# Router scores taken out of the decoder's operands, earlier edge counts, filler matmuls, and a later request for one expert weight

## Chip, core and metric

One core of one Trainium2 chip runs the whole program. The metric is device microseconds of one execution. Engine names are those of the profile: PE (TensorE matmul), PEld (TensorE weight load), DVE (VectorE), ACT (ScalarE), POOL (GpSimd), SP (SyncE, used here as a DMA queue). L1122 is line 1122 of the kernel before.

## What is computed

1250 nodes of 1024 features (10 tiles of 128 rows, the last with 98), 21250 directed edges. Four layers, each added to the stream `x` behind a layer norm:

```python
h = sigmoid(ln(x) @ wenc.T + benc)                       # 500 columns
agg = segment_sum((h @ conv)[src] * edge_weight, dst) + h @ lin.T
x = x + (agg @ wdec.T + bdec)                            # graph layer 1
logits = ln(x) @ wr + br                                 # 4 experts, the best two of each row
x = x + experts_1(ln(x), top2(logits))                   # 1024 -> 512 -> 1024
x = x + gated_relational_layer(ln(x))                    # 8 relations, root, gate
x = x + experts_2(ln(x), argmax(ln(x) @ gate_w.T + b))   # 8 experts, the best one
```

## The kernel before, in words

Every engine has a program of its own; the order is written by hand, and engines meet at semaphores. All weights of the expert and relational layers are split in a high part (ACT, `exp_w[.., k]`, `wh`, `tok_w1h`) and a low part (DVE, the rest), and a product is three matmuls of 512 columns.

**Encoder (0 to 182 us).** DVE sorts the edges by target tile (`sort`, L2058). Between its first and second half it does the layer-norm statistics of all ten tiles (`first_ln`, L2126). ACT normalises (`norm1`), PE transposes (`transpose_x1`), ACT copies back (`take_x1`). The encoder's twelve groups (`q` 0 to 11, L1076) are 8 products each; the groups 8 to 11 are half as wide. PE places 67 of the edge columns in a list by matmul (`permute`, L1059), one behind each product from group 2 on; the other 100 (`SCATTERED`) are written to a table in memory by POOL, one indirect DMA each (L908), and read back by SP (L640). Then PE forms `h @ conv` for ten tiles (L1104), ACT stores it (L1594).

**Edge sums (186 to 415 us).** POOL gathers 176 slots of 128 rows (L917), 16 in flight. PE sums a slot with a one-hot matrix (L1121, L1122), DVE adds it to its tile (L2207). Ten products `h @ lin` lie between the slots (`LIN_AT`).

**Decoder and first router (415 to 507 us).** For each tile PE transposes `agg` (L1126), and forms the 24 matmuls of `decode` (L1128); DVE adds them to `X`, takes statistics; ACT normalises to `ln2_rows`. A tile later PE transposes those rows (`transpose_x2`, L1143), ACT copies them to `XT` (L1635), and two tiles later PE forms 8 products with 4 columns (`route`, L1153); DVE takes the best two three tiles later (`choose0`, L2250). SP stores `ln2_rows` for the gather, and asks for the first weights of experts 1 and 2 only when the last tile is stored and routed (L672 to L676).

**First expert layer (507 to 822 us).** DVE sorts the 2500 pairs into 23 slots, PE turns this into a list (L1185), POOL gathers rows (L925), PE starts at L1203 and L1220. The low parts of the weights are formed by `expert_low` (L2275) in an order written out. The sort does `gate_values` while it waits for PE's counts.

**Relational layer (822 to 2202 us).** Not changed but for its first transpose.

**Second router and expert layer (2202 to 2465 us).** After the last gated tile the route is `transpose_x4`, `route4`, `sort`, the list, four row gathers (L1000), and 17 slots of `up` and `down`. SP asks for expert 0's first and second weights (L845, L851), then for slot 1's first weights, bias, second weights and second bias (L855 to L858), then for slot 2's first weights (`next_w1(0, 0)`, L875). SP takes its instructions in order.

Of the kernel before, what the change touches and what calls it, by code (L numbers as in the profile page):

```python
# [21 lines left out]
F32 = mybir.dt.float32  # L22
# [8 lines left out]
P = 128  # L31
# [16 lines left out]
SCATTERED = 100  # L48
# [56 lines left out]
LN1_AFTER = {0: (4, 5), 1: (6,), 2: (7,), KE: (8,), KE + 1: (9,)}  # L105
# [14 lines left out]
T_AGG = T_LN1 + 2 * NT  # L120
# [12 lines left out]
V_ROUTE = V_DEC + 2 * NT  # L133
V_PRE0 = V_ROUTE + 1
# [44 lines left out]
def build(nc, a, out):  # L179
    ctx = ExitStack()  # L180
    with ctx:
# [162 lines left out]
        hot1 = place("hot1", "hot", [P, RING, P], BF16)  # L344
        hotr = sb("hotr", [P, RING, REL], BF16)
# [12 lines left out]
        b_route = sb("b_route", [P, E0])  # L358
        w_route2 = sb("w_route2", [P, KD, E1])
# [81 lines left out]
        sum_iota = banks[4][:, 0:P]  # L441

# [79 lines left out]
        u2_out = os_kept[1:4] + [(x_in[1], 16), (x_in[2], 16)]  # L522
        t3_out = [(parts_in[k], 32 * len(range(k, NT, 4))) for k in range(4)] + os_kept[0:1]
        c21_out = [(edges_in, 64), (consts_in, 16 * 7), (list_in, 16)]
# [11 lines left out]
        x4_full, xT4_ready, X4 = exp_x_full, exp_xT_ready, 2 * NT + 2 * ESLOTS  # L536
# [68 lines left out]
        def _(sp):  # L605
# [4 lines left out]
            for i in range(2):  # L610
                lo, hi = (0, 4) if i == 0 else (4, NT - 1)
                sp.dma_start(X[:, lo:hi, :], tiles[:, lo:hi, :]).then_inc(x_in[i], 16)

            sp.wait_ge(pad_zero, 1)
            sp.dma_start(X[0:LAST, NT - 1, :], a["x"][(NT - 1) * P:N_NODES, :]).then_inc(x_in[2], 16)
# [9 lines left out]
            sp.dma_start(w0, wide(a["encT"])).then_inc(s0, 16)  # L625
            w1, s1 = unit(UNIT_CONVLIN)
# [9 lines left out]
            sp.wait_ge(room_zero, 1)  # L636
            sp.dma_start(list_dram[0:P * SLOTS0, :].rearrange("(p s) c -> p (s c)", s=SLOTS0), room[:, 0, 0:2 * SLOTS0]).then_inc(list_zero, 16)
# [19 lines left out]
            def load_hidden(s):  # L657
                sp.wait_ge(*hid_stored(s))
                if s < 2:
                    sp.wait_ge(exp_x_full, 2 * NT + 2 * (ESLOTS - 2) + 2)  # L660
                else:
                    sp.wait_ge(exp_hl_ready, 1 + s - 1)
# [5 lines left out]
            first_weights(0, raw[:])  # L668
            for m in range(NT):
# [186 lines left out]
            load_b1(e, 1)  # L856
            load_w2(e, new, 1)
# [25 lines left out]
        def _(pool):  # L883

            pool.memset(X[96:P, NT - 1, :], 0.0).then_inc(pad_zero, 1)
# [14 lines left out]
            pool.memset(room[:], 0.0).then_inc(room_zero, 1)  # L900
# [2017 lines left out]
```

## Time and profile before

| | us |
|---|---|
| median of 3 executions | 2465.64 (2461.29 to 2466.44) |
| the profiled execution's own time | 2467.0 |
| its span in the profile | 2465.1 |
| mean granted TensorE clock | 0.974 |

| engine | busy us | share |
|---|---|---|
| PE | 2315.0 | 94% |
| PEld | 1772.4 | 72% |
| DVE | 1648.0 | 67% |
| ACT | 987.9 | 40% |
| POOL | 858.3 | 35% |

The span is one execution on the core. A busy share is a mean over stages with different limits, so it says which engine is full on the whole and not what a stage waits for.

### The profile page before, as it was taken

The numbers are of one execution on the slowest core, as the hardware profiler recorded it, in microseconds if no ns is written. First come the engines' busy times: TensorE is split into PE (matmuls) and PEld (weight loads), VectorE is DVE, ScalarE is ACT, GpSimd is POOL, SyncE is SP. The second block draws the span as 40 slices with busy tenths as digits, with TensorE's granted clock in tenths as the row PEclk, the third lists the DMA queues.
The fourth block names the chain that finished last, engine by engine and source line by source line (L and its number), as shares of the span: only waits on it lengthen the run. The fifth ranks groups of instructions, "written<-read, shape, count | busy, mean of one in ns | idle before, by whom it ended". The sixth has DMA issues, their size and how long they took to land.

```text
span 2465.1 us, 30737 instructions
## 1 busy us (share of the span) xinstructions
PE 2315.0 (94%) x10060; PEld 1772.4 (72%) x10060; DVE 1648.0 (67%) x2581; ACT 987.9 (40%) x1745; POOL 858.3 (35%) x835
## 2 busy tenths in 40 slices
PE   6998998979999799999999999999999898986998
PEld 3553334868877587888888888887778676875886
DVE  9726777465664576554554555558889889976656
ACT  3112223344343443122121222237889896444333
POOL 2767774011112256545400000034445551103443
PEclk9999999979999899999999999999999998988999
DMA  4027776155454575435435345368678894458884
GB/s 161 2 80 205 209 207 183 64 210 150 116 182 163 179 263 196 151 128 200 141 119 210 122 145 177 123 225 269 213 263 294 293 342 148 158 181 290 306 307 156
DMA packets 195410, 464.06 MB, mean 188 GB/s; under 512 B 29576, under 2 KB 30344, under 8 KB 195288
## 3 DMA queue, kind: packets, MB, share of 16 engines
q1 hardware_dynamic: 98248, 213.30, 24.8%
q0 software_dynamic: 63632, 188.10, 23.9%
q10 hardware_dynamic: 33408, 61.13, 6.6%
q8 instruction: 65, 1.06, 0.2%
q14 instruction: 57, 0.47, 0.1%
HBM read 362.09 MB, written 105.97 MB: 190 GB/s over the span
## 4 chain that ended last, share of the span: by engine, by line
PE 84%; DMA 6%; DVE 5%; issue 2%; ACT 2%; POOL 1%; DVEq 0%; ACTq 0%; SPq 0%; POOLq 0%
PE pair L1367 9%; PE pair L1368 9%; PE pair L1369 9%; PE pair L1122 5%; PE pair L1085 3%; PE pair L1104 3%; PE pair L1385 3%; PE pair L1388 3%; PE pair L1405 2%; PE pair L1407 2%; PE pair L1406 2%; PE pair L1253 2%; PE pair L1254 2%; PE pair L1255 2%; PE pair L1220 2%
## 5 line engine op out<-in xcount | busy, mean ns | idle before, releaser
L1536 ACT ACTIVATE sq_h<-quad 128x512 fp32r<-128x512 f32 x196 | 122.9, 634 | 453.6 <-PE pair L1369 448.8
L1367 PE MATMUL pair<-sq_h,xh 128*128 128x512 f32 x700 | 273.3, 390 | 2.7 <-DVE sq_l L2547 2.7
L1368 PE MATMUL pair<-sq_h,xl 128*128 128x512 f32 x700 | 273.0, 390 | 0.0
L1369 PE MATMUL pair<-sq_l,xh 128*128 128x512 f32 x700 | 272.9, 390 | 0.0
L976 POOL DMA_INDIRECT rows_y<-y_rows,l_row x184 | 196.1, 1066 | 212.8 <-PE pair L1388 189.2
L2635 DVE SCALAR_TENSOR_TENSOR low_y<-rows_y,l_inv,high_y 128x1024 fp32r<-128x1024 f32 x184 | 233.9, 1284 | 41.8 <-ACT high_y L1536 41.6
L1536 ACT ACTIVATE high_y<-rows_y,l_inv 128x1024 fp32r<-128x1024 f32 x184 | 210.3, 1143 | 35.8 <-PE pair L1388 22.1
L953 POOL DMA_INDIRECT inv_ring<-inv_count,at_ring x184 | 189.4, 1029 | 70.9 <-issue 52.4
L2547 DVE TENSOR_TENSOR sq_l<-quad,sq_h 128x512 fp32r<-128x512 f32 x196 | 131.4, 696 | 96.7 <-ACT sq_h L1536 95.9
L917 POOL DMA_INDIRECT XT<-h_rows,l_src x176 | 169.0, 960 | 66.2 <-issue 34.4
L1122 PE MATMUL pair<-XT,XN 128*128 128x504 f32 x352 | 178.9, 633 | 0.0
L1367 PEld LDWEIGHTS pair<-sq_h,xh 128*128 128x128 f32 x700 | 131.7, 188 | 31.0 <-DVE sq_l L2547 3.6
L2207 DVE TENSOR_TENSOR U<-pair,U 128x512 f32 x176 | 121.4, 690 | 46.6 <-DVE U L2207 22.3
L967 POOL COPY X<-bias_u 128x1024 f32<-128x1024 f32 x10 | 10.7, 1127 | 406.4 <-PE pair L1369 406.4
L1369 PEld LDWEIGHTS pair<-sq_l,xh 128*128 128x128 f32 x700 | 131.8, 188 | 27.5
L1368 PEld LDWEIGHTS pair<-sq_h,xl 128*128 128x128 f32 x700 | 131.8, 188 | 27.4
L1385 PE MATMUL pair<-high_y,hot 128*128 128x512 f32 x368 | 117.4, 400 | 18.0 <-DVE low_y L2635 17.9
L1405 PE MATMUL pair<-wh,xh 128*128 128x512 f32 x320 | 125.8, 393 | 2.8 <-DVE wl L2662 2.5
L1407 PE MATMUL pair<-wl,xh 128*128 128x512 f32 x320 | 124.9, 390 | 0.0
L1406 PE MATMUL pair<-wh,xl 128*128 128x512 f32 x320 | 124.9, 390 | 0.0
L1536 ACT ACTIVATE XN<-hot,l_w 128x128 f32<-128x128 bf16 x176 | 57.0, 390 | 161.4 <-DVE hot L2194 161.0
L908 POOL DMA_INDIRECT list_rows<-e_rows x100 | 96.2, 962 | 70.8 <-DVEq L2150 40.7
(402 smaller groups left out, 5583.0 us busy)
## 6 DMA issues: line engine op xcount, KB each, us to landing
quad<-in_L_gnn_weight SPq DMA_DIRECT2D x28, 1024.0 KB, 5.6
xh<-sum_parts SPq DMA_DIRECT2D x14, 1280.0 KB, 7.6
xl<-sum_parts SPq DMA_DIRECT2D x14, 1280.0 KB, 11.2
y_rows<-u ACTq DMA_DIRECT2D x70, 256.0 KB, 2.3
tok_raw<-in_L_ffn_w SPq DMA_DIRECT2D x8, 2048.0 KB, 11.4
tok_raw<-in_L_ffn_w SPq DMA_DIRECT2D x16, 1024.0 KB, 13.5
x_rows<-X SPq DMA_DIRECT2D x20, 512.0 KB, 6.5
pair<-pair_rows SPq DMA_DIRECT2D x18, 512.0 KB, 5.9
```

Of the source, the lines that this page charges most:

```text
L953: pool.indirect_dma_start(inv_ring[:, k:k + 1], None, inv_rows, bass.IndirectOffsetOnAxis(ap=at_ring[:, 0, k:k + 1], axis=0)).then_inc(inv ...
L976: pool.indirect_dma_start(rows_y[s % RING1][:], None, y_rows, bass.IndirectOffsetOnAxis(ap=l_row8[:, s:s + 1], axis=0)).then_inc(y_in[s % ...
L1122: mm(sum_bank[s % 4][:, 0:EMBC], hot[:, s % RING, :], rows_h2[:, s % RING0, 0:EMBC], start=True, stop=True).then_inc(slot_summed, 1)
L1367: mm(o, high[:, k, :], sq_h[:, k, :], start=(k == 0), stop=False)
L1368: mm(o, low[:, k, :], sq_h[:, k, :], start=False, stop=False)
L1369: last = mm(o, high[:, k, :], sq_l[:, k, :], start=False, stop=(k == KE - 1))
L1385: mm(o[:, cols], hot_s, high[:, cols], start=first, stop=False)
L1405: mm(o, xh[:, m, k, :], wh[:, k, :], start=(k == 0), stop=False)
L1406: mm(o, xl[:, m, k, :], wh[:, k, :], start=False, stop=False)
L1407: last = mm(o, xh[:, m, k, :], wl[:, k, :], start=False, stop=(k == KD - 1))
L1536: return nc.scalar.activation(dst, src, func, **kw)
L2635: v.scalar_tensor_tensor(low_y[s % RING1][:], rows_y[s % RING1][:], l_inv[:, s:s + 1], high_y[s % 3][:].bitcast(F32), ALU.mult, ALU.subtra ...
```

## The change

- **Edge list:** 108 instead of 100 columns are scattered by POOL, 59 instead of 67 go through PE. PE's columns start at group 3. POOL's wait for the list's columns is looser.
- **Start:** the node tiles are asked for as tile 0, tiles 1 to 3, (zeroed list, encoder weights), tiles 4 to 8, tile 9. Only tiles 0 to 3 have their statistics inside the sort; 4 to 6 follow the scatter's release, 7 to 9 stand among the columns. ACT's square roots of tiles 5 to 9 now stand between sigmoids. `slot_groups` moves behind the columns.
- **Scores, linear part of `x`:** the router's 4 columns are copied into unused columns 500 to 503 of the encoder's weights, so that the encoder's fourth column group also gives `ln(x) @ wr`. ACT copies that group out (`stage_sc`), PE transposes it (`turn_scores`), ACT keeps `route_x1`.
- **Scores, decoder part:** while the first rows are awaited PE transposes the decoder's weights (32 transposes, 8 copies by ACT), and during slots 16 to 47 forms `wdec.T @ wr` in 32 small matmuls. `decode` then adds 8 matmuls of 8 columns to each tile (high and low parts). DVE adds both parts, and turns them into logits with the tile's mean and root (`choose0`, one tile later).
- **Gone:** `transpose_x2`, its copies to `XT`, `route`.
- **Weights:** expert 2's first weights are asked for together with expert 0's; expert 1's when all tiles are stored. The sort does two `expert_low` pieces where it did `gate_values`; `gate_values` goes behind `expert_x_low(1)`, and all of expert 1's low parts behind it.
- **Filler:** `keep_busy(n)` is n float32 matmuls of 128x128 whose result nobody reads: 16 behind the pair counts (L1180), 12 ahead of `expert_rows(0)`, 16 ahead of `transpose_x3(0)` once the first pairs are in, 9 ahead of and 5 behind `transpose_x4(9)`, 30 behind the second sort's counts (L1469), 30 ahead of `transpose_rows(0)` (L1521).
- **Second expert layer:** slot 1's second weights are asked for when the rows of slots 0 and 1 have landed.

```diff
-SCATTERED = 100
+SCATTERED = 108
-LN1_AFTER = {0: (4, 5), 1: (6,), 2: (7,), KE: (8,), KE + 1: (9,)}
+LN1_AT = {(1, 7): 4, (2, 3): 5, (2, 7): 6, (3, 3): 7, (5, 7): 8, (6, 7): 9}
+COLUMNS_FROM = 3
+STATS_AT, SCALES_AT = {2: (7,), 8: (8,), 10: (9,)}, {6: (7,), 18: (8, 9)}
+SCORES_AT = (KE + 2, 2 * KE)
+SUMS_AT, DEC_SCORES_AT, PARTS_AT = 8, 16, 52
...
             sp.wait_ge(slot_summed, RING0 + SLOTS0)
             first_weights(0, raw[:])
+            first_weights(2, exp_raw[0][:])
...
-            sp.wait_ge(exp_x_full, 2 * NT)
             first_weights(1, exp_raw[1][:])
-            sp.wait_ge(a_full, A_ROUTE + NT)
-            first_weights(2, exp_raw[0][:])
...
             load_b1(e, 1)
+            sp.wait_ge(*tok_rows_here(0))
+            sp.wait_ge(*tok_rows_here(1))
             load_w2(e, new, 1)
...
+            def keep_busy(times, bank=banks[0]):
+                for _ in range(times):
+                    mm(bank[:, 0:P], before[:], ones[:], start=True, stop=True)
+            def turn_scores(g):
+                pe.wait_ge(a_read, A_ENC + KE * (g + 1))
+                transpose4(T_SC + g, [stage_sc[:, q * P:(q + 1) * P] for q in range(TOKG[g][1] // P)])
...
+                    if q == KE - 1:
+                        pe.wait_ge(a_read, 1)
-                        if q >= A_ENC + 2:
+                        if q >= COLUMNS_FROM:
                             next_column()
-                    transpose_x1(LN1_AFTER.get(q, ()))
+                        if (q, k) in LN1_AT:
+                            transpose_x1((LN1_AT[q, k],))
+                    if q in SCORES_AT:
+                        turn_scores(SCORES_AT.index(q))
...
+            pe.wait_ge(w_in[0], 32)
+            for r in range(KD):
+                ...
+                for c in range(KE):
+                    last = nc.tensor.transpose(turn_bank[r % 3][:, c * P:(c + 1) * P], dec_raw[:, c, r // 4, (r % 4) * P:(r % 4 + 1) * P], ident[:])
+            def dec_scores(n):
+                c, k = divmod(n, KD)
+                mm(dec_route_bank[:, c * E0:(c + 1) * E0], dec_turned[:, k, c * P:(c + 1) * P], w_route[:, k, :], start=(k == 0), stop=(k == KD - 1))
...
                         mm(o, agg_h[:, m % 2, k, :], dec_h[:, k, h, :], start=(k == 0), stop=False)
+                        if h == 0:
+                            mm(score_bank[m % 2][:, 0:2 * E0], agg_h[:, m % 2, k, :], dec_route[:, k, :], start=(k == 0), stop=False)
                         mm(o, agg_l[:, m % 2, k, :], dec_h[:, k, h, :], start=False, stop=False)
+                        if h == 0:
+                            score = mm(score_bank[m % 2][:, 0:2 * E0], agg_l[:, m % 2, k, :], dec_route[:, k, :], start=False, stop=(k == KE - 1))
...
-                if m >= 1:
-                    transpose_x2(m - 1)
-                if m >= 2:
-                    route(m - 2)
-            route(NT - 2)
-            transpose_x2(NT - 1)
-            route(NT - 1)
...
+            takes_after = {1: (4,), 2: (5, 6), 5: (8,), 6: (9,)}
+            norms_after = {1: (5, 6), 2: (7,), 3: (8, 9)}
...
+                    if c == KE - 1:
+                        if g >= 1:
+                            act.wait_ge(t_full, T_SC + g)
+                        copy(stage_sc[:, 0:n], enc_bank[q % 4][:, 0:n])
...
+            def take_score(m):
+                dve.wait_ge(a_full, A_ROUTE + m + 1)
+                link(v.tensor_tensor(route_x1[:, m, :], score_bank[m % 2][:, 0:E0], route_x1[:, m, :], ALU.add))
+                v.tensor_tensor(route_x1[:, m, :], score_bank[m % 2][:, E0:2 * E0], route_x1[:, m, :], ALU.add).then_inc(a_read, 1)
             def choose0(m):
-                v.tensor_tensor(logits[:, m, 0:E0], score_bank[m % 2][:, 0:E0], b_route[:], ALU.add).then_inc(a_read, 1)
+                dve.wait_ge(rstd_tile_ready, NT + m + 1)
+                link(v.scalar_tensor_tensor(route_tmp[:, m, :], route_consts[:, 0:E0], nmr[:, m:m + 1], b_route[:], ALU.mult, ALU.add))
+                link(v.scalar_tensor_tensor(logits[:, m, 0:E0], route_x1[:, m, :], rstd[:, m:m + 1], route_tmp[:, m, :], ALU.mult, ALU.add))
...
-            expert_low(in_raw, 2, range(2, KD))
-            expert_low(in_place[1], 1, range(0, 4))
+            expert_low(in_raw, 2, range(4, KD))
             expert_x_low(0)
             expert_x_low(1)
-            expert_low(in_place[1], 1, range(4, KD))
+            gate_values()
+            expert_low(in_place[1], 1, range(KD))
```

## Rows read from the trace of the kernel before

**Rows 1.** The page: the chain that ended last, by engine.
```profile
PE 84%; DMA 6%; DVE 5%; issue 2%; ACT 2%; POOL 1%; DVEq 0%; ACTq 0%; SPq 0%; POOLq 0%
```
**Rows 2.** Timeline of the encoder (start us, busy us, engine, line, count, [idle before <-releaser]).
```profile
29.32 9.12 PE L1085 MATMUL pair<-XT,W 128*128 128x512 f32 x16 [0.78 <-ACT XT L1536]
...
38.52 1.28 ACT L1581 ACT_TABLE_LOAD   x1 [6.47 <-PE pair L1085]
...
41.14 1.06 PE L1038 MATMUL pair<-ident,XN 128*128 128x128 f32 x8 [1.82 <-ACT XT L1536]
...
42.04 7.03 PE L1085 MATMUL pair<-XT,W 128*128 128x512 f32 x16
...
50.64 0.75 PE L1061 MATMUL pair<-room 128*128 128x352 f32 x2
...
147.84 34.57 PE L1104 MATMUL pair<-W,U 128*128 128x512 f32 x80 [0.61 <-issue]
...
179.72 0.25 DVE L2177 TENSOR_SCALAR l_row<-l_row 128x176 f32<-128x176 int32 x1
```
**Rows 3.** POOL's scatters (L908) and gathers (L917): duration ns, first and last start.
```profile
L908 POOL DMA_INDIRECT list_rows<-e_rows x100: 957/962/1125, 47.3 to 172.7; - x100
...
L917 POOL DMA_INDIRECT XT<-h_rows,l_src x176: 945/949/1208, 186.5 to 407.9; - x176
```
**Rows 4.** Busy time in windows (PE, PEld, DVE, ACT, POOL, granted clock, DMA share, GB/s).
```profile
300.00:320.00 20.00, 19.33 (x57) 7.32 (x56) 15.21 (x26) 6.25 (x18) 15.31 (x16) 1.00 0.71 209
...
460.00:480.00 20.00, 20.00 (x122) 17.51 (x121) 10.53 (x30) 6.42 (x11) 0.00 (x0) 1.00 0.20 79
...
2228.00:2240.00 12.00, 3.36 (x11) 2.73 (x12) 1.38 (x2) 1.20 (x2) 4.70 (x5) 0.50 1.04 394
```
**Rows 5.** Timeline of the decoder's first and last tiles.
```profile
418.34 0.50 PE L1138 MATMUL pair<-dec_h,agg_h 128*128 128x512 f32 x1 [1.39 <-DVE agg_l L2043]
...
496.00 1.04 PE L1150 MATMUL pair<-ident,ln_rows 128*128 128x128 f32 x8
...
496.87 3.63 PE L1158 MATMUL pair<-w_route,XT 128*128 128x4 f32 x32
```
**Rows 6.** Timeline from the last decoder product to the first gathered rows.
```profile
498.41 0.16 DVE L2056 SCALAR_TENSOR_TENSOR nmr<-mv,rstd 128x1 f32<-128x1 f32 x1
...
502.39 3.57 PE L1158 MATMUL pair<-w_route,XT 128*128 128x4 f32 x16 [0.69 <-ACT XT L1536]
...
506.48 0.16 DVE L2255 FIND_INDEX8 top_at<-top,logits 128x8 uint32<-128x8 f32 x1
...
521.30 0.94 POOL L925 DMA_INDIRECT exp_rows<-xn_rows,exp_list  x1 [112.47 <-DVEq L2341]
```
**Rows 7.** Timeline of the first expert slots.
```profile
502.51 3.88 SPq L650 DMA_DIRECT2D exp_raw<-in_L_ffn_w  x2
...
512.63 4.27 ACT L1536 ACTIVATE exp_w<-exp_raw 128x512 fp32r<-128x512 f32 x8 [4.62 <-DMA exp_raw<-in_L_ffn_w]
...
528.63 0.79 PE L1220 MATMUL pair<-exp_w,exp_x 128*128 x1 [0.96 <-DVE exp_x L2353]
...
534.17 0.69 DVE L2353 TENSOR_TENSOR exp_x<-pair,exp_x 128x512 fp32r<-128x512 f32 x1 [2.74 <-ACT exp_x L1536]
```
**Rows 8.** Timeline: first product behind the pairs' gather, in the relational layer.
```profile
841.62 0.80 PE L1308 MATMUL pair<-wh,xh 128*128 128x512 f32 x1 [2.00 <-DVE xl L2043]
```
**Rows 9.** Timeline of the second expert layer's start.
```profile
2213.38 4.26 ACT L1536 ACTIVATE tok_w1h<-tok_raw 128x512 fp32r<-128x512 f32 x8 [6.40 <-DMA tok_raw<-in_L_ffn_w]
...
2226.98 0.95 POOL L991 DMA_INDIRECT tok_rows<-xn_rows,tok_list  x1 [43.89 <-DVEq L2800]
...
2235.22 1.94 PE L1482 MATMUL pair<-ident,tok_rows 128*128 128x128 f32 x8 [10.31 <-DMA tok_rows<-xn_rows,tok_list]
...
2238.58 0.80 PE L1491 MATMUL pair<-tok_w1h,tok_xh 128*128 128x512 f32 x1 [1.41 <-DVE tok_xl L2816]
...
2256.12 4.27 ACT L1536 ACTIVATE tok_w1h<-tok_raw 128x512 fp32r<-128x512 f32 x8
```

More of the change, by code:

```diff
@@ L119 @@
 T_LN1 = 0
-T_AGG = T_LN1 + 2 * NT
+T_SC = T_LN1 + 2 * NT
+T_DEC = T_SC + len(TOKG)
+T_AGG = T_DEC + KD
+SCORES_AT = (KE + 2, 2 * KE)
+ROUTE_AT = EMB
+SUMS_AT, DEC_SCORES_AT, PARTS_AT = 8, 16, 52
+assert DEC_SCORES_AT >= SUMS_AT + BATCH + 4 and PARTS_AT >= DEC_SCORES_AT + KE * KD
 T_LN3 = T_AGG + NT
@@ L132 @@
 V_DEC = 1
[L133 to L134 removed]
+V_PRE0 = V_DEC + 2 * NT
 V_LIST0 = V_PRE0 + 1
@@ L1096, in _ @@
             pe.wait_ge(a_read, last_enc)
+            turn_scores(len(TOKG) - 1)
             w = unit(UNIT_CONVLIN)
@@ L1594, in _ @@
                 act.dma_start(h2_dram[m * P:(m + 1) * P, :], OS[:, k, :]).then_inc(os_out[k], 16)
+            for r in range(KD):
+                act.wait_ge(t_full, T_DEC + r + 1)
+                copy(dec_turned[:, r, :], turn_bank[r % 3]).then_inc(t_read, 1)
             for s in range(SLOTS0):
+                if s == PARTS_AT:
+                    act.wait_ge(slot_summed, RING0 + DEC_SCORES_AT + KE * KD)
+                    copy(dec_route[:, :, 0:E0], dec_route_bank.rearrange("p (c e) -> p c e", e=E0))
                 if s % BATCH == 0:
@@ L1625, in _ @@
             agg_high(0)
-            for m in range(NT + 2):
+            for m in range(NT + 1):
                 if m + 1 < NT:
@@ L2117, in _, with first_stats, first_tiles @@
             v.tensor_scalar(tok_pad[:], tok_id[:], float(N_NODES + 1), 100.0, ALU.is_ge, ALU.mult)
+            def first_stats(m):
+                if m in (0, 1):
+                    dve.wait_ge(x_in[m], 16)
+                if m == 4:
+                    dve.wait_ge(x_in[2], 32)
+                ln_stats(m).then_inc(x_tile_ready, 1)
+            def first_tiles():
+                for m in range(4):
+                    first_stats(m)
+                    if m >= 1:
+                        tile_scale(m - 1, 0)
+                tile_scale(3, 0)
             dve.wait_ge(edges_in, 64)
@@ L2260, in _ @@
                     agg_low(m + 1)
-                if m >= 3:
-                    choose0(m - 3)
+                if m >= 1:
+                    choose0(m - 1)
                 for h in range(2):
@@ L2287, in _ @@
                 v.tensor_scalar(pair_id[:, k * NT:(k + 1) * NT], tok_id[:], float(TOP0), float(k), ALU.mult, ALU.add)
-            for m in range(NT - 3, NT):
-                last = choose0(m)
-            link(last)
-            v.sem_inc(v_read, 1)
+            link(choose0(NT - 1))
             link(v.tensor_copy(top_f[:], top_at[:]))
@@ L2302, in gate_values @@
                 link(v.tensor_tensor(gsm[:, 4, :], gsm[:, 3, :], gsm[:, 1, :], ALU.mult))
-            sort(pair_key[:], E0, PT, pair_hot[:], pair_cum[:], pair_pos[:], v_bank[V_PRE0 % 2], V_PRE0, pair_tmp[:], pair_far[:], gate_values, least=E0)
+            sort(pair_key[:], E0, PT, pair_hot[:], pair_cum[:], pair_pos[:], v_bank[V_PRE0 % 2], V_PRE0, pair_tmp[:], pair_far[:], lambda: expert_low(in_raw, 2, range(0, 2)), least=E0)
             link(v.tensor_copy(pair_posi[:], pair_pos[:]))
```

202 lines of the change are left out of this document (125 added, 77 removed).

## Prediction

> **What bounds the kernel now.** I read the chain by engine first: 84% of it is PE [rows 1], so a stretch can be shortened only where PE has less to do, or where something else is in the chain. The timeline then shows three stretches that the change touches. Up to 182.4 us PE runs through: the encoder from 29.3, and 80 matmuls of `h @ conv` that begin at 147.84 and take 34.57 [rows 2]. From 186.5 to 407.9 POOL issues 176 gathers, one each 221.4/175 = 1.265 us [rows 3]; PE is 19.3 of 20 us busy in a window of it, DVE 15.2 [rows 4], so the gathers bound it and PE has about 3% to spare. From 418.3 to 496.0 PE is full while DVE has 10.5 of 20 and ACT 6.4 [rows 4, 5]: PE bounds the decoder. Behind it come chains with PE nearly idle, to the first expert product at 528.63 [rows 6, 7], and from the last router to 2238.58 [rows 9].
>
> **The front.** Products of 512 columns lie 7.03/16 = 0.44 us apart, so a column of the list (two matmuls of 352) costs 0.59 [rows 2]; eight fewer save 4.7. ACT normalises tile 0 after two statistics, not three; I estimate 1.5 earlier, of a first product at 29.32 that ended a wait for ACT [rows 2]. Against it: before, PE stood 1.82 at the transpose behind group 0, for a table load of 1.28, a sigmoid and a copy [rows 2]. Now the same wait lies behind group 2, once more with a load, and with one more copy ahead of it (2.9), and about 0.8 ahead of tile 5: 1.9 more. Three `turn_scores` are 10 transposes of 1.06/8 = 0.13 [rows 2], with waits for the sigmoid and an extra copy by ACT: 2.3. Sum: -4.7 -1.5 +1.9 +2.3 = **-2.0** (from -3.5, if the loads fall into idle time, to +2, if each of six switches between root and sigmoid is met). Scatters: 108 end 8 x 1.27 = 10.1 later by their own pace [rows 3], and start 6 layer norms and the slot numbers earlier, more than that. The list was ready at 180.0, h2 at 182.4 [rows 2], so the gathers hang on h2: they start at 184.5.
>
> At the roots and sigmoids the rows show 1.28 us for a table load and nothing behind it [rows 2]. [...]
>
> **Edge sums: 0.** The pace of 1.265 stays. The 32 transposes (4.2 us at 0.13) and 8 copies of ACT lie in the 4 us between the first gather's issue and its landing, and in what follows; the decoder's weights are asked for behind the scatters, near 171. The 32 score products are 64 matmuls near 0.11, 7 us, in a stretch where PE has 3% of slack: it falls behind by some 6, which 16 rows in flight (20 us) hide, and which the other 128 slots give back. If it isn't given back, up to +5.
>
> **Decoder.** Removed before its last product: 8 times `transpose_x2` at 496.87 - 496.00 = 0.87, and 7 routes at 3.63/2 = 1.8: 19.6. Added: 80 small matmuls. Their price isn't in the trace; the nearest are the route's of 4 columns in the same place, 3.63/32 = 0.113 [rows 5]: 9.0. Ends: 0.02 (hidden in its neighbour), and the 0.22 that the same route takes at 502.39 (3.57/16) [rows 6]. Sum **-10.6** (-18 to -2). Per tile PE then needs about 6.8, DVE by my count 5.7 (its 5 us of before, two additions, one step more in `choose0`), so PE stays the bound, and its waits stay short. ACT loses 1.1 per tile.
>
> **Behind the last product (496.0).** Before, its rows were transposed and routed, the route ended at 502.39 + 3.57 = 505.96, the choice at 506.64: 10.6. Now the choice needs only the statistics, whose scale is there at 498.57 [rows 6], two additions and `choose0`: about 1.25 more, 3.8 in all. **-6.8.** The sort itself is the same, its two `expert_low` pieces end where PE's counts come: +0.2. The filler behind the counts (16 of two matmuls at 0.11 to 0.22, about 5) fits in the 6 that PE waits there. So the first row gather goes from 521.3 to 521.3 - 2.0 - 10.6 - 6.8 + 0.2 = 502.1.
>
> **First expert slots.** Expert 1's weights can only be asked for when the last tile is stored, some 6.5 behind the last product: 483.4 + 6.5 = 489.9. Before, the same request went out at 502.51 and was there at 512.63, 10.1 later; ACT takes 4.27 for each of two experts [rows 7]: 489.9 + 10.1 + 8.5 = 508.5, and only then `exp_x`, which the rows want at 507.7. About +1. DVE then does 8 pieces and `gate_values` between its second and its third `exp_x`; it idled 2.74 there before [rows 7]. Together **+1.5** (0 to +4). The 23 slots behind are PE's own and unchanged.
>
> **First relational product: 0.** At 841.62 it waits for DVE, not for PE [rows 8]; faster transposes leave it there. The filler of some 5 us starts with the pairs and ends with the first normalised tile: -1.9 to +0.8.
>
> **Second expert layer.** The filler around `transpose_x4(9)` shortens the route by up to 2, but DVE's sort does two low pieces that wait for ACT, and ACT for a load that lands at 2213.38 [rows 9]: 0. The gathers are issued at 2226.98 in both. [...] With the 2 MB of second weights out of the way I take 5, so they are there at 2232. [...] Queued behind SP's new wait are the second weights, a bias and slot 2's first weights: two requests of 2 MB from 2233 on at 394 GB/s [rows 4], beside 1.5 MB of rows, are there by 2249; slot 2's are used at 2256.1 - 2.9 = 2253.2. That cover is 4 us.
>
> **Sum.** -2.0 -10.6 -6.8 +0.2 +1.5 -2.9 = -20.6. The profiled execution took 2467.0 (span 2465.1), so it would take 2446.4; it stood 1.4 above the median of 2465.64, which gives **2445.0**.
>
> **Rivals.**
> - *Front and start both lose:* the table switches and score transposes eat the columns' gain (+2 in place of -2), expert 1's weights come 2.5 later, DVE's packed order holds slot 2. For it: ACT gets six more loads, and its race at 508 has no slack. Against: ACT was idle 6.5 us around the first load. -20.6 + 4 + 2.5 = -14: 2451.5. Chance 0.20.
> - *Each switch costs its load twice:* the wait behind group 2 and the one ahead of tile 5 grow by 1.3 each, -18: 2447.7. Against: the next ACT row begins when the load ends [rows 2]. [...] Chance 0.08.
> - *Small matmuls nearly free:* they hide under their 512-column neighbours, DVE's 5.7 becomes the tile time less waits, and the filler gains more. -20.6 - 8 = -28.6: 2437. For it: five of six neighbours are long. Chance 0.13.
> - *The filler doesn't do what it is for:* the clock still stands at half where real work starts, and only the earlier landing counts, with the rows behind the filler: -2.9 becomes 0. 2448. Chance 0.12.
> - [...] If DVE's chain (decoder sum, statistics, score, scale, choice) is nearer 9 than 5.7 a tile, PE idles over 2 us in each; behind 0.7 us of idleness and short matmuls the route at 502.39 ran at half rate [rows 6], while at 418.34, behind 1.4, products ran at full rate [rows 5]. Ten tiles of 6.8 would take twice as long: -20.6 + 68 - some overlap = +40, 2505. [...] Against: DVE's count. Chance 0.03.
>
> **Numbers.** Forecast 0.44, rivals as above. The bounds of the unknown costs, not all at once, reach 2436 to 2456, and that takes in all but the slower case. A measurement of this kernel tells 0.2% (about 5 us) from no change. All cases but the last and a tail of the first (0.02, within 0.2%) are faster by more: 0.95, 0.02, 0.03.
>
> **What would show it.** First gather near 184.5 and the last 221 later; decoder tiles 6.8 apart; last decoder product to first expert gather in 18.7, not 25.3; first expert product 18 to 19 earlier than 528.63; first `tok_rows` landing in 5, and PE at 0.23 spacing at once. Wrong would be: gathers that wait for sums (PE the bound there), PE idle between decoder tiles, `exp_x` behind ACT's weights by over 3, slot 2 of the last layer waiting for its weights.

## The result and the profile after

The kernel after takes 2443.14 us in the median of 4 runs (2441.12 to 2448.11), the kernel before 2466.04 beside it (2461.29 to 2469.06): ratio 0.9922, 95% interval 0.9905 to 0.9939, 22.9 us by the medians. Forecast were 2445.0 and 2436 to 2456. The profiled execution took 2441.12, its span is 2439.3, mean granted clock 0.984 (0.974 before). The spans differ by 25.8.

The first table cuts them at events that both traces have. "Measured" is how much each stretch of after is longer than that of before; the last column is my term for it.

| stretch | before | after | measured | forecast |
|---|---|---|---|---|
| start to first row gather of the edge sums | 186.51 | 179.57 | -6.9 | -2.0 |
| first to last gather of the edge sums | 221.37 | 223.54 | +2.2 | 0 |
| last gather to first decoder product | 10.46 | 10.27 | -0.2 | 0 |
| that to the last decoder sum read | 77.86 | 69.53 | -8.3 | -10.6 |
| that to the last choice of experts | 10.28 | 3.31 | -7.0 | -6.8 |
| choice to first expert gather | 14.82 | 14.57 | -0.2 | +0.2 |
| gather to first expert product | 7.33 | 7.91 | +0.6 | +1.5 |
| first expert product to first gather of layer 2 | 1698.35 | 1695.48 | -2.9 | 0 |
| that gather to the end | 238.12 | 235.12 | -3.0 | -2.9 |
| sum | | | -25.8 | -20.6 |

The sum was missed by 5.2: by 4.9 in the first row, while the misses of the other rows (+2.2, +2.3, -2.9, -0.9 and smaller ones) nearly cancel. In after PE has 78% of the chain by engine, DMA 9% (84% and 6% in [rows 1]).

**Front.** Timeline of after (start us, busy us, engine, line, operation, count, idle before and its releaser). PE's row of 139.69 answers to 147.84 in [rows 2], POOL's first gather to [rows 3].

```profile
4.46 0.25 DVE L2203 TENSOR_SCALAR U<-U 128x167 int32<-128x167 int32 x1 [0.42 <-DMA U<-in_edge_weight]
...
35.85 1.28 ACT L1641 ACT_TABLE_LOAD   x1
...
37.15 0.69 ACT L1641 ACTIVATE U<-pair,b_enc 128x512 f32<-128x512 f32 x1
...
44.36 1.09 PE L1058 MATMUL pair<-ident,XN 128*128 128x128 f32 x8 [0.78 <-ACT XN L1589]
...
50.24 1.06 PE L1058 MATMUL pair<-ident,XN 128*128 128x128 f32 x8 [1.36 <-ACT XT L1581]
...
139.44 0.41 PE L1058 MATMUL pair<-ident,stage_sc 128*128 128x128 f32 x2 [1.04 <-ACT U L1641]
139.69 34.50 PE L1138 MATMUL pair<-W,U 128*128 128x512 f32 x80
...
168.55 0.43 SPq L661 DMA_DIRECT2D dec_raw<-in_decT  x1
...
174.85 0.33 ACTq L1661 DMA_DIRECT2D h_rows<-OS  x1
...
177.54 5.38 PE L1156 MATMUL pair<-ident,dec_raw 128*128 128x128 f32 x32 [3.36 <-DMA dec_raw<-in_decT]
...
179.57 0.97 POOL L937 DMA_INDIRECT XT<-h_rows,l_src  x1 [12.55 <-DMA h_rows<-OS]
```

DVE begins on the edges at 4.46, not at 6.66; PE waits for ACT at 44.36, 50.24 and 139.44 (and once for 0.34); the last rows of `h @ conv` are stored at 174.85 and gathered from 179.57, 4.7 later, where before it was 186.51 - 183.08 = 3.4.

**Decoder and choice.** Timeline of after, its last decoder tiles, and windows at its first (columns as in [rows 4]).

```profile
469.69 0.69 DVE L2370 TENSOR_TENSOR X<-X,pair 128x512 f32<-128x512 f32 x1 [1.32 <-PE pair L1204]
...
476.53 0.69 DVE L2370 TENSOR_TENSOR X<-X,pair 128x512 f32<-128x512 f32 x1 [1.31 <-PE pair L1204]
...
480.19 0.69 DVE L2370 TENSOR_TENSOR X<-X,pair 128x512 f32<-128x512 f32 x1 [0.29 <-PE pair L1204]
...
482.91 0.69 DVE L2370 TENSOR_TENSOR X<-X,pair 128x512 f32<-128x512 f32 x1 [1.30 <-PE pair L1204]
...
486.22 0.16 DVE L2358 FIND_INDEX8 top_at<-top,logits 128x8 uint32<-128x8 f32 x1
```

```profile
413.00:415.00 2.00, 1.62 (x5) 1.38 (x6) 0.93 (x2) 0.00 (x0) 0.00 (x0) 0.67 0.92 310
415.00:417.00 2.00, 2.00 (x7) 1.68 (x6) 0.00 (x0) 0.00 (x0) 0.00 (x0) 0.50 1.01 372
```

Half tiles without small matmuls are 482.91 - 480.19 = 2.72 long, one with 8 of them 480.19 - 476.53 = 3.66: 0.117 for each, where 0.113 was forecast. A tile that also transposes the next sums takes 476.53 - 469.69 = 6.84, 6.8 by the forecast. The first tile ran at half clock for about 3.7 us, where before, behind the same wait of 1.39, it ran at full rate [rows 5].

**First expert slots and second expert layer.** Timelines of after; they answer to [rows 6, 7] and [rows 9].

```profile
489.21 0.38 SPq L669 DMA_DIRECT2D exp_raw<-in_L_ffn_w  x1
...
498.82 8.43 ACT L1581 ACTIVATE exp_w<-exp_raw 128x512 fp32r<-128x512 f32 x16 [6.58 <-DMA exp_raw<-in_L_ffn_w]
...
507.15 1.06 ACT L1581 ACTIVATE exp_x<-pair 128x512 fp32r<-128x512 f32 x2
...
508.70 0.79 PE L1258 MATMUL pair<-exp_w,exp_x 128*128 x1 [1.92 <-DVE exp_x L2454]
...
2204.05 9.34 PE L1066 MATMUL pair<-ones,before 128*128 128x128 f32 x60 [2.96 <-DVEq L2901]
2204.18 0.95 POOL L1011 DMA_INDIRECT tok_rows<-xn_rows,tok_list  x1 [44.34 <-DVEq L2901]
...
2211.67 1.49 SPq L839 DMA_DIRECT2D tok_raw<-in_L_ffn_w  x2
...
2213.22 1.04 PE L1526 MATMUL pair<-ident,tok_rows 128*128 128x128 f32 x8
...
2215.83 0.50 PE L1535 MATMUL pair<-tok_w1h,tok_xh 128*128 128x512 f32 x1 [1.57 <-DVE tok_xl L2917]
...
2224.73 0.47 PE L1535 MATMUL pair<-tok_w1h,tok_xh 128*128 128x512 f32 x1 [1.62 <-DVE tok_w1l L2933]
```

The weights of expert 1 were asked for at 489.21 (489.9 forecast) and their pieces end at 507.15 with `exp_x` right behind them, the race as drawn, 1.3 earlier. In the second layer the filler ends at 2213.4, though SP, which waits for the rows of both slots, was let go by 2211.67.

### The profile page after: what moved, and what is told of

The parts are those of the page before. It is cut to its first block, busy times and chain, and to the rows that moved or that the text cites. A ratio compares the mean times of both kernels' runs of the same rounds, so it can differ in the third digit from the quotient of the medians.

```text
span 2439.3 us, 31100 instructions
## 1 busy us (share of the span) xinstructions
PE 2322.1 (95%) x10228; PEld 1791.2 (73%) x10228; DVE 1639.1 (67%) x2596; ACT 993.3 (41%) x1747; POOL 864.7 (35%) x843
## 4 chain that ended last, share of the span: by engine, by line
PE 78%; DMA 9%; DVE 5%; issue 3%; ACT 2%; POOL 2%; DVEq 0%; SPq 0%; ACTq 0%; POOLq 0%
PE pair L1408 9%; PE pair L1409 9%; PE pair L1410 9%; PE pair L1179 5%; DMA tok_x<-x_rows,tok_list 5%; PE pair L1426 3%; PE pair L1429 3%; PE pair L1138 3%; PE pair L1115 3%; PE pair L1446 3%; PE pair L1447 3%; PE pair L1448 3%; PE pair L1291 2%; PE pair L1292 2%; PE pair L1293 2%
## 5 line engine op out<-in xcount | busy, mean ns | idle before, releaser
L928 POOL DMA_INDIRECT list_rows<-e_rows x108 | 103.9, 962 | 59.5 <-issue 32.3
```

## The experiments

Each run has a median of 4 timed runs (10 in the first), and a ratio to the kernel before from the same chip. Single executions of one kernel lie up to 12 us apart, so the traces' stretches carry most verdicts, and medians only what is over 3 us. Lines in the rows are those of each variant.

**1. POOL's zeroing of `room`.** The change shortens it from 4096 columns to 352, in a line that the diff above leaves out, and my forecast has no term for it. In the kernel before:

```diff
-            pool.memset(room[:], 0.0).then_inc(room_zero, 1)
+            pool.memset(room[:, 0, 0:2 * SLOTS0], 0.0).then_inc(room_zero, 1)
```

> The kernel before, with one edit: POOL zeroes only the 352 columns of `room` that are copied to the list, not all 4096. Theory A (two engines slow each other): the two small DVE operations that took 3.50 and 3.31 us beside the 3.51 us memset take under 0.4 each, DVE starts on the edges at about 4.5 instead of 6.66, and the first encoder product comes at 27.2 instead of 29.32; the kernel is about 2 us faster. Rival B (DVE waited for the edge loads, which land near 4.4 or 6.6 whatever POOL does): DVE's edge work starts at 6.6 still, and the time is unchanged.

Timeline of the kernel before, and of this one:

```profile
3.14 3.51 POOL L900 MEMSET room<- 128x4096 f32 x1
3.23 3.50 DVE L2116 TENSOR_SCALAR before<-iota_free,iota_part 128x128 f32<-128x128 f32 x1 [2.05 <-POOL ident L898]
3.43 3.31 DVE L2117 TENSOR_SCALAR tok_pad<-tok_id 128x10 f32<-128x10 f32 x1
```

```profile
3.13 0.39 POOL L900 MEMSET room<- 128x352 f32 x1
3.23 0.38 DVE L2116 TENSOR_SCALAR before<-iota_free,iota_part 128x128 f32<-128x128 f32 x1 [2.04 <-POOL ident L898]
...
4.21 0.25 DVE L2121 TENSOR_SCALAR U<-U 128x167 int32<-128x167 int32 x1 [0.59 <-DMA U<-in_edge_weight]
```

Measured: theory A for the mechanism. The two DVE operations fall from 3.50 and 3.31 to 0.38 and 0.19, edge work starts 2.45 earlier, the first product comes at 27.76 (1.6 earlier), the first gather at 184.16 (2.4), the last decoder sum 1.65 earlier. Not all of the 2.4 is the memset: the encoder of this execution also began at full rate, its first 16 products taking 2.0 less than in [rows 2], and the last store of `h @ conv` was gathered from 4.7 behind it and not 3.4.

```profile
27.76 7.10 PE L1085 MATMUL pair<-XT,W 128*128 128x512 f32 x16 [0.78 <-ACT XT L1536]
```

But the choice comes at 506.43 against 506.48, and the time is 2463.44, ratio 0.9993 (0.998 to 1.0007). In its trace the end of the router stands at half rate for longer than in [rows 5, 6] (the last 32 products ahead of them took 4.62, not 3.63, and the last transposes 1.95, not 1.35): the 1.65 us went there. In the kernel after that piece of PE work is gone.

The reverse, in the kernel after: a second memset behind `ident`.

```diff
+            pool.memset(room[:, 1:4, :], 0.0).then_inc(more_zero, 1)
...
             v.sem_inc(scatter_ready, 1)
+            dve.wait_ge(more_zero, 1)
```

> The kernel after, with a second memset of POOL over the other 3072 columns of `room`, put where the large one was before. Theory A: the memset takes 2.6 us, the two small DVE operations last as long as it, edge work begins 1.5 to 2 later than 4.46, the first encoder product comes at 27 instead of 25.30, 1.5 to 2 us lost in all. Rival B: DVE is untouched by it, first product at 25.3, no loss.

Measured: memset 2.66 at 3.58, DVE's two operations 2.65 and 2.46, edge work from 6.24, first product at 26.91, `h @ conv` from 141.29, first gather at 180.96: 1.8, 1.6, 1.6 and 1.4 later than after. The median, 2442.17, doesn't show it. So the memset is worth 1.6 us at the first product in either direction, and 1.4 at the first gather where nothing else changed; in the total it is below what I can tell.

**2. The second layer's filler and SP's wait.** Four variants of the kernel after. The first leaves out the last `keep_busy(30)`, the third and fourth make it 15; the second and fourth leave out SP's wait:

```diff
-            sp.wait_ge(*tok_rows_here(0))
-            sp.wait_ge(*tok_rows_here(1))
...
             pe.wait_ge(tok_list_ready, 1)
-            keep_busy(30)
+            keep_busy(15)
```

> The kernel after without the last filler, 30 times two passes of PE behind the list of the second expert layer. Theory A (the filler ends after the rows have landed, so it costs as much as it gives): the transposes start when the rows land, about 7.4 us behind the first gather instead of 9.0, but cold, 1.94 long, and slot 0's first products at 0.43 spacing; the first product stands where it stood, 11.6 behind the gather, and slot 1's first product comes 1.3 to 1.6 later; 1.5 us slower in all. Rival B (the filler is worth what I forecast, 0.95 for the transposes and 1.5 for the products, and costs nothing): 2.5 slower. Rival C (the earlier rows alone count): no change or 1 faster.

> The kernel after, without SP's wait for the rows of slots 0 and 1 ahead of slot 1's second weights. Theory A (the rows land about 1 us later, and the filler, which ends 1.6 after them, hides that): the first rows land 8 us behind the gather instead of about 7.4, slot 0's transposes stay at 9.0 behind it, and the time is within 0.5 us of the kernel after. Rival B (my forecast: rows take 5 with the wait and 8 without): start unchanged at the first slot, since the filler covers it, but the rows of slot 1 late by 1 or 2, so up to 1 us slower. Rival C (the wait costs, since the second weights come late): up to 1.5 us faster, by what PE waits at slot 1's first products now.

> The kernel after with 15 in place of 30 fillers in front of the second expert layer. Without them the transposes began 5.59 us behind the first gather, with 30 of them 9.04. Theory A (the filler overshoots the rows by 3.4, and a shorter one keeps the clock as well): the filler takes 5.5, the transposes start 5.6 to 6 behind the gather and are 1.04 long, first product 8.3 behind it (11.65 now), slot 0's products at 0.23 spacing, slot 1's first product 17.1 to 17.5 behind the gather (20.55 now); 3 us faster than the kernel after. Rival B (15 are too few to raise the clock by the time real work starts): the transposes start at 5.6 but slot 0 runs at 0.43 spacing, slot 1 at 20.5 behind the gather, no gain.

> The same shorter filler, and SP's wait ahead of slot 1's second weights taken away. Theory A (the wait lets the rows land in 5.6 instead of about 8, and this is now uncovered): transposes 8 to 8.5 behind the gather, 2.5 later than with the wait, so 2 to 2.5 us slower than the kernel with 15 fillers and the wait. Rival B (the rows' landing is not what the second weights delay): same start as with the wait, same time.

PE's timelines behind the first gather: without filler (gather at 2206.36), with 15 (2209.77; the fourth row is DVE's), and with 15 and no wait (2204.72):

```profile
2211.95 1.94 PE L1526 MATMUL pair<-ident,tok_rows 128*128 128x128 f32 x8 [8.67 <-DMA tok_rows<-xn_rows,tok_list]
2215.30 0.80 PE L1535 MATMUL pair<-tok_w1h,tok_xh 128*128 128x512 f32 x1 [1.41 <-DVE tok_xl L2916]
```

```profile
2209.65 6.07 PE L1066 MATMUL pair<-ones,before 128*128 128x128 f32 x30 [2.96 <-DVEq L2901]
2215.55 1.08 PE L1526 MATMUL pair<-ident,tok_rows 128*128 128x128 f32 x8
2218.20 0.50 PE L1535 MATMUL pair<-tok_w1h,tok_xh 128*128 128x512 f32 x1 [1.57 <-DVE tok_xl L2917]
...
2226.27 4.89 DVE L2933 TENSOR_TENSOR tok_w1l<-tok_raw,tok_w1h 128x512 fp32r<-128x512 f32 x8
...
2227.10 0.47 PE L1535 MATMUL pair<-tok_w1h,tok_xh 128*128 128x512 f32 x1 [1.62 <-DVE tok_w1l L2933]
```

```profile
2213.02 1.97 PE L1524 MATMUL pair<-ident,tok_rows 128*128 128x128 f32 x8 [2.51 <-DMA tok_rows<-xn_rows,tok_list]
2216.40 0.80 PE L1533 MATMUL pair<-tok_w1h,tok_xh 128*128 128x512 f32 x1 [1.41 <-DVE tok_xl L2915]
```

All columns are us behind the first gather; "last slot" is the first `down` product of slot 16.

| fillers | SP waits | transposes | slot 1's first product | slot 2's first product | last slot | end |
|---|---|---|---|---|---|---|
| 0 (before) | no | 8.24 | 21.99 | 36.1 | 222.0 | 238.1 |
| 0 | yes | 5.59 | 20.59 | 34.8 | 220.7 | 235.1 |
| 30 | no | 8.74 | 20.25 | 32.8 | 218.6 | 234.8 |
| 30 (after) | yes | 9.04 | 20.55 | 34.8 | 220.6 | 235.1 |
| 15 | yes | 5.78 | 17.33 | 29.8 | 215.7 | 231.8 |
| 15 | no | 8.30 | 22.12 | 36.1 | 222.0 | 238.1 |

Up to slot 1's first product each half alone gives 1.4 to 1.7 us and both together give 1.4 as well, for the 30 fillers last 9.3 and the rows, with SP's wait, 5.6. With 15, which end as the rows land, the two add up to 4.7, and without the wait all is lost again: PE idles 2.5 and is cold (granted clock 0.50, transposes 1.97). The mechanism of theory A held in all four, its sizes in two. In the first the first product came 2.7 earlier than in after, slot 0 at half rate (its first products 0.43 apart, 0.23 in after) took that back, and nothing was lost, where 1.5 were forecast. In the fourth the loss is 6.3 and not 2.5: 4.8 at slot 1's first product, since I left out that the clock falls too, and the rest behind it.

To the end the gains look like 3, 3, 3 and 6.3, but two more things are in these numbers, and neither was planned. The first is another meeting of POOL and DVE. From slot 1's first product to slot 2's it takes 12.5 in the second and third variant, and 14.0 to 14.2 in the others, before and after included. In after POOL adds a bias to `tok_x` while DVE forms the low parts of slot 1's first weights: one of DVE's eight pieces lasts 2.87 instead of 0.68, all eight 7.08 instead of the 4.89 of the variant with 15, and PE waits 1.46. With 15 fillers these pieces end before that addition begins; with 30 and no wait they do too, for its rows land later. In the kernel before and in the fourth variant it falls on the low parts of the second weights, and one piece of these lasts 2.65 to 2.79. In the second and third variant it falls on them as well, but there POOL's addition is what lasts longer (5.63 and 7.01), and DVE keeps its pace (4.89); what decides between the two isn't shown. Timeline of after:

```profile
2223.91 7.08 DVE L2933 TENSOR_TENSOR tok_w1l<-tok_raw,tok_w1h 128x512 fp32r<-128x512 f32 x8
...
2226.78 2.46 POOL L1031 TENSOR_TENSOR tok_x<-tok_x,U 128x1024 f32<-128x1024 f32 x1 [3.09 <-DMA tok_x<-x_rows,tok_list]
...
2229.84 0.50 PE L1535 MATMUL pair<-tok_w1h,tok_xh 128*128 128x512 f32 x1 [1.46 <-DVE tok_w1l L2933]
```

The second is the clock in the last slot. From its first `down` product, always behind a wait of 2.05 or 2.06, to the end it is 14.5 in nine of the fourteen traces and 16.1 in five (before, three of these variants, and the first of experiment 7). The kernel before has both (14.5 in experiment 1), and so has the shorter filler with the wait, so it is chance. Windows in it, of before and of after (columns as in [rows 4]):

```profile
2450.00:2453.00 3.00, 3.00 (x9) 2.33 (x8) 0.00 (x0) 0.00 (x0) 1.01 (x1) 0.50 0.05 8
```

```profile
2426.00:2429.00 3.00, 3.00 (x15) 2.48 (x14) 0.69 (x1) 0.00 (x0) 1.01 (x1) 1.00 0.03 3
```

The medians, 2443.91, 2440.82, 2441.62 and 2445.22, are too coarse for this: on one chip the first two differ by 3.1, where their traces differ by 0.4 from the gather on, and on another the last two by 3.6, where it is 6.3. The intervals of their ratios overlap.

**3. The decoder's weights.** They were asked for at 168.55, behind the scatters. Here at 138.08:

```diff
+            sp.wait_ge(a_full, A_H2)
+            sp.dma_start(dec_raw[:]..., wide(a["decT"])).then_inc(w_in[UNIT_DEC % 2], 16)
             sp.wait_ge(scattered, 16 * SCATTERED)
...
-            sp.wait_ge(a_full, A_H2)
-            sp.dma_start(dec_raw[:]..., wide(a["decT"])).then_inc(w_in[UNIT_DEC % 2], 16)
```

> The kernel after with the decoder's weights asked for before SP waits for the scatters, at about 140 instead of 168.5. Theory A (the first gather waits for the last rows of `h @ conv`, whose store is held up behind the 2 MB of weights; it came 4.7 behind the store where the weights landed last and 2.9 where the store was issued after them): the gather comes 2.4 to 3 behind the last store, at 177.3 if the encoder starts warm (h @ conv from 139.7) and 179.5 if cold (from 141.8); up to 2.3 us faster. Rival B (a store takes 3 to 4.7 there by its own chain of stores): gather stays 4.7 behind the store. In both the list is not the bound, ready at 171.7.

Timeline of this variant, the last store of `h @ conv` and the first gather:

```profile
174.50 0.33 ACTq L1661 DMA_DIRECT2D h_rows<-OS  x1
...
177.37 0.98 POOL L937 DMA_INDIRECT XT<-h_rows,l_src  x1 [10.29 <-DMA h_rows<-OS]
```

Measured: theory A. The store at 174.50 is gathered from at 177.37, 2.9 later. The three variants of experiment 2 whose encoder began cold bear it out without any edit there: their store left as the weights landed, and was gathered from 2.9 later too. The median is 2437.87, ratio 0.9892 (0.9872 to 0.9913), whose interval overlaps that of after, so the gain is read from the store and the gather alone. So in the kernel after the front's end is set by 2 MB of weights that land first.

**4. No filler at all.** `keep_busy` does nothing.

> The kernel after without any of its six fillers. Theory A (each filler only warms what follows it): counts to first expert gather unchanged (14.6 us from the choice) or up to 1.5 longer, by the list's products at half rate; first expert product within 1 of where it is; last route of the second router 1.2 slower, at half rate; list of the second layer 1 slower; start of slot 1 as without the last filler. Together 2 to 4 us slower than the kernel after. Rival B (the fillers are worth nothing, since DVE's chain sets these places): within 1 us of it.

Measured: 2448.73, ratio 0.9931; its profiled execution 2452.48. Choice to first expert gather 14.56, to the first expert product 7.89: both as in after, so up to there the fillers buy nothing. The last router tile of layer 2 is back at half rate (PE's timeline of this variant; its 16 score products take 3.58 as in before, 1.85 in after):

```profile
2194.29 3.58 PE L1478 MATMUL pair<-w_route,xT 128*128 128x8 f32 x16 [0.69 <-ACT xT L1580]
...
2211.19 2.30 PE L1516 MATMUL pair<-tok_perm_val,tok_perm_lane 128*128 128x18 f32 x10 [9.94 <-DVE tok_perm_val L2891]
```

That is 1.2 from the norm to the choice, and 1 at the list. From the gather to the end it is 235.15, as without the last filler. Its first gather came at 182.43, 7.0 behind the store, for the decoder's weights took 12.4 us to land: that is not the fillers' doing. The median is 5.6 above that of after, but from another chip; by the ratios to the kernel before, 0.9931 and 0.9922, it is 2.2, with overlapping intervals. A's 2 to 4 fits, and isn't shown by the total.

**5. The list's columns.** `SCATTERED = 100` in the kernel after.

> The kernel after with 100 scatters, so 67 columns of the list on PE instead of 59. Theory A (8 columns of 0.59 lie on the way to `h @ conv`): from the first encoder product to the first of `h @ conv` 4.7 more (119.1 if warm at the start, 121.4 if cold; 114.4 or 116.8 with 108); the scatters end 10 earlier, so the decoder's weights are asked for at 158 and have landed long before the last store: the first gather comes 2.9 behind the store and not 4.7, so 2.9 us later in all and not 4.7. Rival B (columns hide in the waits for ACT): 1 to 2 more only.

Measured: from the first product to `h @ conv` 146.57 - 25.00 = 121.57, against 116.7 to 116.8 in the three executions with 108 scatters whose encoder began cold too: 4.8. Theory A, 4.7 forecast. The store at 181.74 was gathered from at 184.60, 2.9 behind. The median is 2446.02, ratio 0.9914 (0.9898 to 0.9931), beside the 0.9922 of after: the total doesn't show the loss.

**6. What the score products cost the edge sums.** 28 of 32 are left out, so the router sees another sum and picks other experts; only the gathers are read.

```diff
-                if DEC_SCORES_AT <= s < DEC_SCORES_AT + KE * KD:
+                if DEC_SCORES_AT <= s < DEC_SCORES_AT + KE * KD and (s - DEC_SCORES_AT) % KD == 0:
```

> The kernel after with 4 of the 32 score products in the edge sums; 28 are left out, so the router scores lack 7/8 of the decoder's part and the choice of experts is another. Only the stretch from the first to the last gather is read. It took 221.4 in the kernel before and 223.2 to 223.5 in the kernel after and its variants. Theory A (64 small passes of PE put its sums behind, and the gathers wait for a free row twice): two long gaps between gathers, near 200 and 217, shrink from 1.6 and 2.1 to 1.4 or less, and the stretch is 222.3 or less. Rival B (the transposed decoder weights and the copies that share ACT set it): unchanged, 223.3.

Measured: 223.01, so neither: the gap at 217 shrinks from 2.1 to 1.7, the one at 199 to 1.46, and those two are about 0.5 of the 2.2. The whole stretch can't show that, for with all 32 products it lay between 222.87 and 223.70. The kernel before with the small memset took 222.33 for its own gathers, so 1 of the 2.2 comes without the change. The rest wasn't found.

**7. A version that beats both.** First the decoder's weights early and 15 fillers, then also these:

```diff
-SCATTERED = 108
+SCATTERED = 110
...
+            keep_busy(3)
             pe.wait_ge(agg_ready, 1)
...
                 if m + 1 < NT:
                     transpose_agg(m + 1)
+                if m == 0:
+                    keep_busy(5)
                 decode(m)
...
-            keep_busy(12)
+            keep_busy(24)
```

> The kernel after with the decoder's weights asked for at about 140 and with 15 in place of 30 fillers ahead of the second expert layer. Theory: the two gains add, 2.2 from the gathers (the first at 177.4 to 179.6, 2.9 behind the last store) and 3.3 behind the second layer's first gather (231.8 us from it to the end, not 235.1): about 5.5 us faster than the kernel after, 2437 to 2438, ratio to the kernel before 0.989 to 0.990. Rival (what lies between takes back what comes early): 2440 or more, with both stretches as said and the stretch between them longer.

> As the kernel with both edits, and three more: 110 scatters (two columns of the list fewer on PE, 1.2 us), 3 and 5 fillers around the first transposes of the decoder, and 24 in place of 12 ahead of the first expert rows. Theory A: first gather 1.2 earlier (the list is ready at about 174.5, ahead of the rows at 176); the decoder's stretch is 67.9 and not 69.5; the first expert product's neighbours lie 0.23 apart from the start instead of 0.43 for 3.5 us, 1.8 gained; 3 us faster than the kernel with the two edits. Rival B (the clock behind 1.9 us of idleness is low whatever stood ahead): slot 0 at 0.43 again, gain only 1.2. Rival C (the filler overshoots): slot 0's transposes later than 4.5 behind the first gather.

Measured: 2441.06, ratio 0.9882 (0.9864 to 0.9900), and 2433.94, ratio 0.9859 (0.9835 to 0.9883). Against the 0.9922 (0.9905 to 0.9939) of the kernel after, from another chip, the second is faster with room between the intervals; those of the first are 0.0005 apart, too little to hang anything on. The intervals of the two variants overlap, so the second isn't shown to beat the first. In the first the total is the rival's and not 2437 to 2438, though both stretches are as said (store to gather 2.9, gather to end 232.1): the decoder took 70.99, its first tile wholly at half clock. Windows around it, in the first and in the second:

```profile
410.00:412.00 2.00, 1.18 (x3) 1.04 (x4) 1.36 (x3) 0.11 (x1) 0.00 (x0) 0.65 0.97 299
412.00:414.00 2.00, 2.00 (x8) 1.66 (x7) 0.00 (x0) 0.00 (x0) 0.00 (x0) 0.50 1.03 375
```

```profile
410.00:412.00 2.00, 1.73 (x11) 1.39 (x10) 1.31 (x3) 0.06 (x1) 0.00 (x0) 1.00 0.89 283
412.00:414.00 2.00, 2.00 (x13) 1.71 (x12) 0.00 (x0) 0.00 (x0) 0.00 (x0) 1.00 1.00 367
```

With the fillers around the first transposes PE is busy 1.73 of 2 us ahead of the tile and stays at full clock: 67.94. Of the eleven traces without these fillers seven had 67.9 as well, so one execution doesn't prove it. The two columns fewer gave their 1.2 between the first product and `h @ conv`, but the first product came 0.7 later, and the first gather only 0.5 earlier. The 24 fillers ahead of the expert rows gave nothing, as rival B has it: behind a wait of 2.58 the first products stood 0.42 to 0.59 apart. PE's timeline of the second variant there:

```profile
504.65 0.79 PE L1261 MATMUL pair<-exp_w,exp_x 128*128 x1 [2.58 <-DVE exp_x L2457]
505.24 0.63 PE L1262 MATMUL pair<-exp_w,exp_x 128*128 x1
505.66 0.63 PE L1263 MATMUL pair<-exp_w,exp_x 128*128 x1
```

## Why the prediction was right, and where it wasn't

The time was right, and not by its parts alone: the front was missed by 4.9, the edge sums and the decoder gave 4.5 of that back, and the second expert layer came out right by two errors that cancel. What the change does to the front, the decoder and the choice of experts is as forecast in kind; that 2445.0 and 2443.14 lie only 1.9 apart is luck.

**Front: -2.0 forecast, -6.9 measured.** Step by step:
- *The first product*, "I estimate 1.5 earlier", came 4.0 earlier. The order of the statistics gave 1.6: from the start of the edge work to the first norm 11.33 became 9.76 (17.99 - 6.66, 14.22 - 4.46). The rest is the memset that the change shortens, which I took for no cost since nothing in the chain waits for POOL there. Edge work starts 2.2 earlier by it, and experiment 1 shows that the memset alone is worth 1.6 at the first product, added or taken away. The 0.8 that is left came only with both.
- *The columns*, -4.7: shown, 4.8.
- *The waits and score transposes*, "+1.9" and "+2.3": 3.52 of waits in place of 1.82, and 10 transposes of 0.11 each: +2.8 instead of +4.2. The scores were priced right (1.38 of waits and 1.1 of transposes), and so was the wait ahead of tile 5 (0.78); the one behind group 2 was 1.36 and not 2.9, for the table load ahead of it (45.46 to 46.74) fell into ACT's idle time.
- *A cold start*, not in my sum: before, the first 16 products took 9.12 where 7.1 is full rate; after, they stood at full rate, 7.10. The granted clock reads 1.00 in both, so this is read from the products: the first ones of before start 0.85 apart, those of after 0.43. That is chance: of the 12 traces of after and its variants that I compared, 8 had 13.97 for the first 32 products and 4 had 16.3 to 16.4. It didn't matter: in those 4, `h @ conv` began at 141.8 to 142.2 (in experiment 5 later, by its columns), yet the first gather at 179.8 to 180.2, beside 179.57.
- *"The gathers hang on h2"* needs its second half: on h2's store, which lands behind the decoder's weights. 1.3 were lost there beside before, and 1.8 beside a store with no load ahead of it (experiment 3).

**Edge sums: 0, measured +2.2.** "It is given back" was wrong: each batch of `h @ lin` products (3.60) holds a gather up (1.16 to 1.79 in after, where the others take 0.95), and with 3% of slack nothing is given back. Two gaps that shrink without the score products are 0.5 of it, 1 is spread; the bound of +5 held.

**Decoder: -10.6, measured -8.3.** The prices held (0.117 for 0.113; tiles 6.8). Of the 2.3 missed, 1.6 is the clock at the first tile and 0.3 the price; 0.4 has no owner. Eight of 12 traces of after and its variants have 67.9, thus -9.9.

**Behind the last product: -6.8, measured -7.0; sort and first slots +1.7, measured +0.3.** Right, with ACT's race as drawn.

**Relational product: 0.** It waited 2.87 for DVE after, 2.00 before [rows 8], and came 3.97 behind the start of its transposes in both; nothing gained.

**Router of layer 2: 0, measured about -1.2.** I gave the warm last tile to ACT's load. From the last norm to the choice it is 2211.13 - 2203.08 = 8.05 before, 2186.76 - 2179.91 = 6.85 after, and experiment 4 takes it back. The other 1.7 of that row of the table can't be assigned: in the variants that change nothing in it, this stretch lay between 1689.7 and 1702.1.

**Second expert layer: -2.9, measured -3.0.** The number is right by luck. The -2.9 is 0.5 for an earlier start, 0.95 for warm transposes (1.94 against 1.06) and 1.5 for first products 0.23 and not 0.43 apart. The rows landed in 5.6 to 5.7, 5 by the forecast, 8.1 before, where DMA was full and the granted clock 0.50 [rows 4]. But the transposes began 0.8 later behind the gather than before, where they were to gain 0.5. That 0.5 rests on my estimate of how long 30 fillers take, which no run shows: they took 9.34. The warm transposes gave 0.75 (0.95), slot 0 at full rate 1.5 (1.5), so slot 1's first product came 1.44 earlier and not 2.9. The other 1.6 is the clock in the last slot, half in before and full in after (experiment 2), of which my sum knew nothing. And one cost that is in both kernels wasn't seen: POOL's addition beside DVE's low parts, 1.6. I saw the filler outlast the rows; that this makes wait and filler share one gain, and that half the filler gives 3.2 more at slot 1, I did not.

**The rivals.** *Front and start both lose* fell with the front: its load at 45.46 fell into idle time (1.28, with 2.19 of idleness behind it), and expert 1's weights were asked for at 489.21 as drawn. *Each switch costs its load twice* fell too: the load at 35.85 lasts 1.28 and ACT's next row begins at 37.15. Nothing stands between them. *Small matmuls nearly free* fell by 0.117 each. *The filler doesn't do what it is for* is half true: PE is at full rate behind it (transposes 1.04 and not 1.94), and it overshoots. The rival of 2505, ten tiles at half rate, has one such tile in four of the executions, for 1.6 to 3.1 us, and never ten; from how much idleness on the clock falls isn't shown, for all of these stood behind a wait of 1.39 or 1.40.

## What to carry to other kernels

Size a filler by what it covers: one that outlasts the data gives away what it buys, and each further one here costs 0.22 us (15 of them 3.26), so read the data's landing with and without it. Before a gain in a tail is credited to an edit, cut the tail at its waits: of three gains of 3 us here, 1.4 to 1.7 were what the edits were for. A wait that keeps a large load behind small rows is worth its price only if PE is ready when the rows land (here 4.8 us at slot 1's first product with 15 fillers, nothing with 30). And where a store feeds the next stage, look at which megabytes are in flight ahead of it: asking for 2 MB 30 us earlier brought the first gather from 4.7 to 2.9 behind the last store. And look beside DVE's chain for what POOL computes, not only for what DVE waits for: in these kernels POOL held DVE up twice, and the waits of PE behind it name only DVE.

## What the runs showed of the hardware that I had not expected

- A DVE operation of 0.2 to 0.4 us beside a POOL memset lasts until the memset ends: 3.50 beside 3.51, 2.65 beside 2.66, 0.38 beside 0.39. What makes them wait for each other isn't shown.
- The same with two working operations: beside POOL's addition of 128x1024 (2.46) a DVE subtraction of 0.68 lasted 2.87; in two other traces DVE's kept 0.68 beside it and POOL's took 5.63 and 7.01 instead of 2.38 (experiment 2, 30 without the wait and 15 with it).
- The clock behind the same short wait differs from execution to execution: at the decoder's first tile, always behind 1.39 or 1.40, 7 of 11 traces show full rate, three lost 1.6 us and one 3.1; in the last slot, always behind 2.05 or 2.06, nine of 14 show full rate and five lost 1.6. A term of a sum that hangs on such a place had a spread of 1.6 to 3.1 us here, whatever was planned.
- A store of 256 KB, issued with 2 MB of loads in flight, was gathered from 4.5 to 7.0 us later, 3.4 later in the kernel before, where they landed 1.7 behind its issue, and 2.9 later where they had landed or did so within 0.6.
